# A decoder layer on one core: cross attention's sums stored straight into the rows of its output projection, the softmax shares spread by TensorE, the projection moved into the cross-attention stage, and the last down products dealt out

## The chip, the cores and the metric

One core of one Trainium2 chip. The metric is the device time of one execution in microseconds. Times of three runs of the kernel before: 1092.85, 1093.76 and 1097.8 us, median 1093.76.

## What is computed

A pre-norm decoder layer in float32 on x of shape 4 x 1024 x 256, 16 heads of 16. Only the last two of its three blocks matter here:

```python
x = x + self_attention(layernorm(x))
# cross attention, context of 77 rows, boolean mask
q, k, v = heads(layernorm(x) @ Wq), heads(ctx @ Wk), heads(ctx @ Wv)
attn = softmax(where(masked, -1e9, q @ k.T / 4))
x = x + (attn @ v).reshape(b, s, 256) @ Wo
# feed forward, hidden width 768
h = silu(n @ w_gate.T) * (n @ w_up.T)        # n = layernorm(x)
x = x + h @ w_down.T
```

## The kernel before, in words

The work runs in stages on one core: projections of self attention, self attention, a middle stage (its output projection and the queries of cross attention), cross attention (684 to about 849 us of the trace), feed forward (to the end). Tokens are held as 8 chunks of 512 (two to a batch), `xres` holds the residual of every chunk in SBUF. Matrix products that must be accurate are cut into three products of high and low parts (`cut_products`, line 128); line 135 is their one matmul.

**Cross attention** works in 16 groups, each 4 heads of one batch; groups 4b to 4b+3 are batch b. A group has 8 score units u (2 halves of 512 queries x 4 heads). For a unit TensorE makes the scores of 80 keys by 512 queries (lines 1339, 1341), ScalarE their exponentials (1301), and after each four units TensorE multiplies by the values (`products`, 1349). The value tile `vx` has VW = 32 columns to a head, 16 of values and 16 ones, so that a head's 32 rows of the PSUM bank are 16 sums and 16 equal softmax denominators. ScalarE copies them to `xu` (1293) and SP stores all of `xu` to DRAM, `od2` (1214). The maxima that the exponentials subtract are made two groups ahead: eight TensorE products (1324, 1326), each reduced by VectorE (1263), and two transposes `t` (1320) whose result VectorE copies to `xmrow` (1260) and SP moves under the queries (1209). These ten items go round a ring of three PSUM banks, so item N waits for VectorE's reading of item N-3. Their order, and their places between the score units, are the lists `ring2` and `plan2` (lines 1116 to 1130). The queries come by six DMAs to a group, three groups ahead (`load_cross`, 1201). All DMAs of the stage go through SP's one queue, in program order, and SP waits in order too (`cross_sync`, 1206). The weights of feed forward are loaded at groups 0, 1 and 6 (1172) and split by ScalarE and GpSimd (1182, 1184, 1190).

**From sums to projection.** After a batch's four groups SP loads the denominators back (`load_den2`, 1401), VectorE inverts them at the end of group 4b+5 (`inverse`, 1406), SP stores the inverses (1410), and from group 7 on loads sums and inverses, the inverses repeated 16 times, into `oin2` and `din2` (`load_ffn`, 1417, 1419). GpSimd multiplies the two (`quotients3`, 1425), TensorE projects with `xwo` (`project3`, 1454), VectorE adds to `xres` (1436) and takes the moments for the next norm. Chunk 0's projection stands in group 15; those of chunks 1 to 7 stand at the head of the feed-forward iterations.

**Feed forward**, iteration c of 8, on TensorE: the projection of chunk c+1, gate and up products of hidden tiles 2, 3, 4, the transposes of chunk c+1 (`turn`, 1571), tile 5, tiles 0 and 1 of chunk c+1, then the 72 down products of chunk c. A hidden tile goes TensorE, ScalarE (silu, 1549), VectorE (1500, 1502), GpSimd (the low part, 1475). The last iteration has only tiles 2 to 5 and the down products.

Of the kernel before, what the change touches and what calls it, by code (L numbers as in the profile page):

```python
# [29 lines left out]
def program(nc, x, ctx_t, mask_t, Wq, bq, Wk_t, bk, Wv_t, bv, Wo_t, bo, W_cross, shift_w, gate,  # L30
# [35 lines left out]
    od2 = dram("od2", (G, HG, 2, HD, S), F32)  # L66
    rdn2 = dram("rdn2", (G * HG, S), F32)
# [5 lines left out]
    with root:  # L73
# [36 lines left out]
        vx = sb(root, "vx", [SK, B, H, VW])  # L110
# [171 lines left out]
        def qkv_gpsimd(g):  # L282
# [26 lines left out]
            nc.gpsimd.memset(vx[0:S2, :, :, HD:VW], 1.0).then_inc(s_con, 1)  # L309
# [806 lines left out]
        ring2 = [("m", i) for i in range(8)]  # L1116
        ring2.insert(6, ("t", 0))
        ring2.append(("t", 1))
        NMX2, NST2, NPS2, LAG2, AHEAD, LATE2 = len(ring2), 2 * HG, 8, 3, 2, 2

        plan2, at = [], 0
        for u in range(NST2):
            plan2.append(("s", u, 0))
            if u == LATE2:
                plan2.append(("r", NMX2 - 1, AHEAD - 1))
            plan2 += [("p", half, -1) for half in range(2) if HG * (half + 1) - 1 == NST2 + u - LAG2]
            plan2 += [("p", half, 0) for half in range(2) if HG * (half + 1) - 1 == u - LAG2]
            upto = max(0, u + 1 - LATE2) * (NMX2 - 1) // (NST2 - LATE2)
            plan2 += [("r", n, AHEAD) for n in range(at, upto)]
            at = upto  # L1130
# [75 lines left out]
        def cross_sync(sp, first):  # L1206
            def maxima(g, c):
                sp.wait_ge(xs_mxe, g * NMX2 + ring2.index(("t", c)) + 1)
# [12 lines left out]
            for g in range(G):  # L1221
                if g + GB - 1 < G:
# [8 lines left out]
                if g < 2:  # L1231
                    load_weight(sp, g)
                if g == 6:
                    load_weight(sp, 2)
                b = g // GB - 1
                if b >= 0 and g % GB == 1:
                    for w in range(2):
                        sp.wait_ge(xus[w], 16 * 2 * (b + 1))
                    load_den2(sp, b)
                if b >= 0 and g % GB == 2:  # L1240
                    store_inverse(sp, b)
                if 7 <= g < 7 + 2 * KT:
                    load_ffn(sp, (g - 7) // KT, [(g - 7) % KT])
            store(G - 1)

        def cross_gpsimd(g):
            for x in range(3 * NPC):
                ffn_weight_low(g, x)
            for c in range(2):
                quotients3(g, c)  # L1250
            power3(g, 0)

        def cross_vector(v, first):
            def item(g, n):
                kind, m = ring2[n]
                N = g * NMX2 + n
                src = bank[MXB[N % NMB]]
                v.wait_ge(xs_mxf, N + 1)
                if kind == "t":
                    nc.vector.tensor_copy(xmrow[:, g % 2, m], src[0:32, 0:P // 2].bitcast(BF16)).then_inc(xs_mxe, 1)  # L1260
                    return
                half, r = m // 4, m % 4
                nc.vector.tensor_reduce(xpm[:, half, :, r], src[:, 0:HG * SK].rearrange("p (h w) -> p h w", h=HG),  # L1263
                                        AX, ALU.max).then_inc(xs_mxe, 1)
                if r == 3:
                    v.wait_ge(xs_mxe, N + 1)
                    top = xpm[:, half].rearrange("p h r -> p (h r)")
                    nc.vector.tensor_copy(xmt[:, half, 0], top).then_inc(xs_cmb, 1)
                    v.wait_ge(xs_cmb, 2 * g + half + 1)
                    nc.vector.tensor_tensor(xmt[:, half, 1], top, xmt[:, half, 0], ALU.subtract).then_inc(xs_mt, 1)  # L1270

            if first:
                for n in range(AHEAD * NMX2 - 1):
                    item(n // NMX2, n % NMX2)
                return
# [515 lines left out]
```

## Time and profile before

| what | value |
|---|---|
| median of 3 runs | 1093.76 us (1092.85 to 1097.8) |
| the profiled execution's own time | 1098.37 us |
| its span in the trace, first to last instruction | 1096.5 us |
| busy: TensorE, VectorE, ScalarE, GpSimd | 1036.7, 722.4, 577.0, 216.3 us |
| mean granted TensorE clock | 0.956 |
| chain that ended last, share of TensorE | 75% |

The page of the profile gives shares of the whole span; the stages have different limits, so the rows below are taken by stretch. In the trace "idle before <-X" on an instruction is how long its engine stood still before it and what ended that. Matmuls are pipelined: the distance from start to start is their cost, their own duration is longer. A float32 matmul stands as two records.

### The profile page before, as it was taken

The page shows a single profiled execution, that of the slowest core. Times are in us where ns is not written, and L with a number is a line of the kernel's source. Part 1 is how long each engine was busy: PE and PEld are TensorE (multiplying, and loading weights), DVE is VectorE, ACT ScalarE, POOL GpSimd, SP SyncE. Part 2 cuts the span into 40 slices and gives each one's busy share as a digit, 9 for nine tenths or more (in the row PEclk, how much of TensorE's full clock was granted, in tenths as well). Part 3 has the DMA queues.
Part 4 walks back from the last instruction along what each step waited for, and adds up shares of the span by engine and source line. Part 5 has one row for each costly group of instructions (what it writes and reads, how often), then busy time and mean ns, then how long its engine had stood idle before and what let it go on. Part 6 is the DMA issues. An engine that isn't in the chain of part 4 may idle for free.

```text
span 1096.5 us, 18966 instructions
## 1 busy us (share of the span) xinstructions
PE 1036.7 (95%) x7044; PEld 615.4 (56%) x7092; DVE 722.4 (66%) x1571; ACT 577.0 (53%) x1093; POOL 216.3 (20%) x228
## 2 busy tenths in 40 slices
PE   4999799999999999999999998999889999999997
PEld 3877244444444444444444465544334788888886
DVE  7877978777787788887785375655453545445552
ACT  4785167676676676676676577377555211111110
POOL 6655700000000000000000044011020233333431
PEclk9999599999999999999999999699888899999999
DMA  8589604444433344444400237588851111111101
GB/s 252 198 217 313 121 2 80 79 80 80 69 65 59 66 72 74 83 84 79 80 16 15 40 118 174 131 210 190 195 120 64 63 58 58 54 43 49 48 2 38
DMA packets 85511, 105.30 MB, mean 96 GB/s; under 512 B 12548, under 2 KB 73696, under 8 KB 83885
## 3 DMA queue, kind: packets, MB, share of 16 engines
q1 hardware_dynamic: 82907, 100.92, 39.1%
q10 hardware_dynamic: 2514, 3.18, 1.3%
q8 instruction: 56, 0.92, 0.4%
q14 instruction: 34, 0.28, 0.1%
HBM read 61.80 MB, written 37.06 MB: 90 GB/s over the span
## 4 chain that ended last, share of the span: by engine, by line
PE 75%; DVE 15%; ACT 4%; DMA 3%; issue 2%; SPq 1%; POOL 0%; POOLq 0%; DVEq 0%; ACTq 0%
PE bank L135 21%; PE bank L843 11%; PE bank L810 10%; PE bank L829 9%; DVE pm L740 8%; PE bank L1101 3%; PE bank L1454 3%; PE bank L1339 2%; PE bank L1341 2%; PE bank L941 2%; PE bank L1349 2%; PE bank L833 2%; PE bank L1324 2%; PE bank L815 2%; PE bank L1326 2%
## 5 line engine op out<-in xcount | busy, mean ns | idle before, releaser
L787 ACT ACTIVATE prob<-bank 128x512 f32<-128x512 f32 (+1 forms) x608 | 317.7, 584 | 188.5 <-PE bank L833 101.6
L740 DVE TENSOR_REDUCE pm<-bank 128x1 f32<-128x512 f32 (+3 forms) x608 | 356.9, 655 | 87.6 <-PE bank L815 66.8
L810 PE MATMUL bank<-stk,stq 96*128 96x512 bf16 (+3 forms) x768 | 226.1, 338 | 5.1 <-DVE pm L740 2.8
L829 PE MATMUL bank<-stq,stk 98*128 98x512 bf16 (+3 forms) x768 | 222.8, 331 | 2.6 <-ACT prob L787 0.5
L843 PE MATMUL bank<-prob,va 128*17 128x512 f32 (+3 forms) x1536 | 145.5, 497 | 2.5
L810 PEld LDWEIGHTS bank<-stk,stq 96*128 96x128 bf16 x768 | 68.7, 98 | 136.4 <-DVE pm L740 80.2
L1549 ACT ACTIVATE e_sg<-bank 128x512 f32<-128x512 f32 x48 | 28.7, 599 | 189.3 <-PE bank L135 189.3
L1301 ACT ACTIVATE xprob<-bank 80x512 f32<-80x512 f32 x128 | 72.4, 591 | 66.5 <-PE bank L1341 65.1
L961 POOL TENSOR_TENSOR c_rstd<-c_ve,mhalf 128x4 f32<-128x4 f32 x8 | 8.1, 1008 | 500.6 <-DVE c_ve L128 500.6
L829 PEld LDWEIGHTS bank<-stq,stk 98*128 98x128 bf16 x768 | 69.5, 99 | 45.0 <-ACT prob L787 9.2
L1263 DVE TENSOR_REDUCE xpm<-bank 128x4 f32<-128x320 f32 x128 | 58.9, 488 | 37.8 <-PE bank L1326 36.2
L843 PEld LDWEIGHTS bank<-prob,va 128*17 128x17 f32 x1536 | 40.5, 113 | 72.8 <-issue 52.8
L833 PE MATMUL bank<-tri_k,identb 128*128 128x128 bf16 (+1 forms) x335 | 80.3, 240 | 0.0
L135 PE MATMUL bank<-e_xnt,wg 128*128 128x512 f32 x288 | 77.0, 403 | 1.4 <-DVE e_xnt L1507 1.4
L1475 POOL TENSOR_TENSOR e_ht<-e_hf,e_ht 128x512 fp32r<-128x512 f32 x48 | 62.5, 1303 | 73.5 <-DVE e_ht L1502 73.5
L815 PE MATMUL bank<-tri_q,identb 128*128 128x128 bf16 (+1 forms) x321 | 76.0, 237 | 0.0
L135 PE MATMUL bank<-wd,e_ht 128*128 128x256 f32 x576 | 71.8, 286 | 3.2 <-POOL e_ht L1475 3.2
L135 PE MATMUL bank<-e_xnt,wu 128*128 128x512 f32 x288 | 74.5, 395 | 0.0
L135 PEld LDWEIGHTS bank<-wd,e_ht 128*128 128x128 f32 x576 | 71.4, 195 | 4.2 <-POOL e_ht L1475 3.6
L1500 DVE TENSOR_TENSOR e_hf<-bank,e_sg 128x512 f32<-128x512 f32 x48 | 33.1, 690 | 51.2 <-ACT e_sg L1549 51.2
L135 PEld LDWEIGHTS bank<-e_xnt,wg 128*128 128x128 f32 x288 | 54.6, 192 | 12.8 <-DVE e_xnt L1507 1.8
L135 PEld LDWEIGHTS bank<-e_xnt,wu 128*128 128x128 f32 x288 | 54.9, 191 | 11.8
(172 smaller groups left out, 1376.7 us busy)
## 6 DMA issues: line engine op xcount, KB each, us to landing
qk<-a_parts SPq DMA_DIRECT2D x32, 384.0 KB, 2.7
od<-xu SPq DMA_DIRECT2D x16, 512.0 KB, 4.0
xq<-c_parts SPq DMA_DIRECT2D x16, 384.0 KB, 3.1
xstq<-xq SPq DMA_DIRECT2D x32, 192.0 KB, 4.7
stq<-qk SPq DMA_DIRECT2D x30, 192.0 KB, 4.0
stk<-qk SPq DMA_DIRECT2D x15, 384.0 KB, 6.2
vs<-a_vst SPq DMA_DIRECT2D x8, 544.0 KB, 4.2
oall<-u_out SPq DMA_DIRECT2D x64, 64.0 KB
```

Of the source, the lines that this page charges most:

```text
L135: mm = nc.tensor.matmul(dst, a[:, i], b[:, j], start=(n == 0), stop=(n == 3 * len(terms) - 1))
L740: nc.vector.tensor_reduce(pm[:, k, h0:h0 + hb, r], src[:, 0:hb * w].rearrange("p (h w) -> p h w", h=hb), AX, ALU.max).then_inc(s_mxe, 1)
L787: nc.scalar.activation(prob[:, U % NPS, 0:hb * n], bank[STB[U % NSB]][:, 0:hb * n], ACT.Exp).then_inc(s_ex, 1)
L810: mm = nc.tensor.matmul(dst[:, h * w:(h + 1) * w], stq[i][0:R, half, h0 + h, r * P:(r + 1) * P], stk[i][0:R, h0 + h, k0:k0 + w], start=(h ...
L815: mm = nc.tensor.matmul(dst[:, 0:hb * w].rearrange("p (h w) -> p h w", h=hb)[:, :, w - P:w], identb[:], tri_q[:, 0:hb], start=False, stop= ...
L829: mm = nc.tensor.matmul(dst[:, h * n:(h + 1) * n], stk[i][0:RM, h0 + h, kt * P:(kt + 1) * P], stq[i][0:RM, half, h0 + h, q0:q0 + n], start ...
L833: mm = nc.tensor.matmul(dst[:, 0:hb * n].rearrange("p (h n) -> p h n", h=hb)[:, :, 0:P], identb[:], tri_k[:, 0:hb], start=False, stop=True ...
L843: mm = nc.tensor.matmul(bank[PVB[half]][h * VW:h * VW + VC, q0:512], va[g % NB][:, kt, :, h], prob[:, (g * NST + first + h // hb) % NPS, ( ...
L1263: nc.vector.tensor_reduce(xpm[:, half, :, r], src[:, 0:HG * SK].rearrange("p (h w) -> p h w", h=HG), AX, ALU.max).then_inc(xs_mxe, 1)
L1301: nc.scalar.activation(xprob[:, U % NPS2], bank[STB[U % NSB]][0:SK, :], ACT.Exp).then_inc(xs_ex, 1)
L1475: nc.gpsimd.tensor_tensor(ht[:, c % 2, 1, h], hf[:, h % 2], ht[:, c % 2, 0, h].bitcast(F32), ALU.subtract).then_inc(es_hl, 1)
L1500: nc.vector.tensor_tensor(hf[:, h % 2], bank[5 + 2 * (h % 2)][:], sg[:, h % 2], ALU.mult).then_inc(es_h, 1)
```

## The change

- The DRAM tensors `od2` and `rdn2`, their loads and GpSimd's quotients go. `store_sums3` writes each head's 16 rows of `xu` into the projection's rows `oall2` in SBUF, four DMAs of 64 KB to a group, and the denominators by a fifth into `den2`; before it was one DMA of 512 KB.
- The denominators of a batch are inverted and cut into three bfloat16 parts on VectorE (`shares3`), in unit 4 of group 4b+5, stored to DRAM and loaded as 48 rows. TensorE spreads them over the 16 rows of each head (`sel`, a matmul of 512 columns), VectorE multiplies.
- Spreads ("s") and half projections ("o") are items of the ring of three banks. Those of chunks 0 to 5 stand in groups 7, 11 and 15, two chunks to a group; those of chunks 6 and 7 in feed-forward iterations 1 and 2.
- The places of the other ring items shift by at most one within a unit. Chunk 0's moments and norm follow groups 13 and 14 on VectorE.
- The last two weight loads go from groups 1 and 6 to groups 3 and 7. `vx` has 17 columns to a head.
- The last chunk's down products are dealt between its gate and up products, 12 to a hidden tile, each waiting for its own tile.

```diff
+        def cross_items(g):
+            todo = [[] for u in range(NST2)]
+            b, i = g // GB - 1, g % GB
+            if b >= 0 and i == 3:
+                for u in range(2):
+                    todo[4 * u].append(("s", 2 * b + u, 0))
+                    todo[4 * u + 1].append(("s", 2 * b + u, 1))
+                    todo[4 * u + 2].append(("o", 2 * b + u, 0))
+                    todo[4 * u + 3].append(("o", 2 * b + u, 1))
+            if g + AHEAD - 1 < G:
+                todo[LATE2].append(("t", g + AHEAD - 1, 1))
+            if g + AHEAD < G:
+                ring = maxima_of(g + AHEAD)
+                for n, item in enumerate(ring):
+                    todo[LATE2 + n * (NST2 - LATE2) // len(ring)].append(item)
+            return todo
...
-            def store(g):
-                sp.wait_ge(xs_u, 2 * g + 2)
-                sp.dma_start(od2[g:g + 1].rearrange("a h w r t -> (a h w r) t"), xu[:, g % 2]).then_inc(xus[g % 2], 16)
...
                 if g:
-                    store(g - 1)
+                    store_sums3(sp, g - 1)
+                if b >= 0 and i == 1:
+                    store_shares3(sp, b)
                 if g + AHEAD < G:
                     maxima(g + AHEAD, 0)
...
+                if g in (0, 3, 7):
+                    load_weight(sp, (0, 3, 7).index(g))
+                if b >= 0 and i == 1:
+                    load_shares3(sp, b)
...
+                for u, due in enumerate(steps2[g]):
+                    if b >= 0 and i == 1 and u == 4:
+                        shares3(v, b)
...
+                if g == G - 3:
+                    moments3(v, 0)
+                if g == G - 2:
+                    normalise3(v, 0)
...
+                if kind == "s":
+                    t.wait_ge(s_rl2, 16 * (g // 2 + 1))
+                    nc.tensor.matmul(dst[:], sel[:, m], shares_of(g), start=True, stop=True).then_inc(xs_mxf, 1)
+                    return
+                if kind == "o":
+                    t.wait_ge(xs_mxe, place2["s", g, KT - 1] + 1)
+                    project3(dst, g, m).then_inc(xs_mxf, 1)
+                    return
...
+            sp.wait_ge(xs_u, 2 * g + 2)
+            for h in range(HG):
+                row = HD * (HG * (i % 2) + h)
+                sp.dma_start(oall2[row:row + HD, b % 2, i // 2],
+                             xu[h * VW:h * VW + HD, g % 2]).then_inc(xus[g % 2], 16)
+            rows = S // DT * HG
+            sp.dma_start(den2[rows * i:rows * (i + 1), b % 2],
+                         xu[HD:P:VW, g % 2].rearrange("a (c t) -> a c t", t=DT)).then_inc(xus[g % 2], 16)
...
+            nc.vector.reciprocal(den2[:, q], den2[:, q]).then_inc(s_rd2, 1)
+            for part in range(2):
+                v.wait_ge(s_rd2, n + 2 * part + 1)
+                nc.vector.tensor_copy(xr3[:, q, part], den2[:, q]).then_inc(s_rd2, 1)
+                v.wait_ge(s_rd2, n + 2 * part + 2)
+                if part == 0:
+                    nc.vector.tensor_tensor(den2[:, q], den2[:, q], xr3[:, q, 0], ALU.subtract).then_inc(s_rd2, 1)
+                else:
+                    nc.vector.tensor_tensor(xr3[:, q, 2], den2[:, q], xr3[:, q, 1], ALU.subtract).then_inc(s_rd2, 1)
...
             t.wait_ge(s_fl, 3 * NPC)
+            t.wait_ge(xs_mxe, NMX2)
             turn(0)
...
-            for c in range(NCH):
-                more = c + 1 < NCH
-                if more:
-                    project3(t, c + 1)
-                for h in range(2, HT - 1):
+            for c in range(NCH - 1):
+                if c in LATE_AT:
+                    spread3(c - 1)
+                gate_up(c, 2)
+                if c in LATE_AT:
+                    t.wait_ge(es_on, KT * c)
+                    for w in range(2):
+                        t.wait_ge(es_yo, 2 * (c - 1) + w + 1)
+                        project3(bank[OB[w]], N_LATE + c - 1, w).then_inc(es_op, 1)
+                for h in range(3, HT - 1):
                     gate_up(c, h)
...
                 down(c)
+            for h in range(HT):
+                if h + 2 < HT:
+                    gate_up(NCH - 1, h + 2)
+                down_part(NCH - 1, h)
```

## Rows read from the trace of the kernel before

**Rows 1.** The page, granted TensorE clock in 40 slices of 27.4 us.

```profile
PEclk9999599999999999999999999699888899999999
```

**Rows 2.** Busy time and clock by stretch: PE, PEld, DVE, ACT, POOL, PEclk, DMA share, GB/s.

```profile
730.00:738.10 8.10, 8.10 (x78) 3.84 (x74) 4.69 (x14) 6.29 (x13) 1.00 (x1) 1.00 0.76 161
784.00:788.00 4.00, 2.10 (x12) 1.05 (x12) 0.89 (x2) 1.08 (x2) 0.00 (x0) 0.59 0.97 224
841.40:1096.50 255.10, 243.98 (x1367) 212.77 (x1365) 123.12 (x265) 42.05 (x73) 84.74 (x62) 0.97 0.14 46
```

**Rows 3.** TensorE's timeline, the product with the values in several groups: start, us.

```profile
703.97 1.06 PE L1349 MATMUL bank<-xprob,vx 80*32 80x512 f32 x8
...
729.15 1.06 PE L1349 MATMUL bank<-xprob,vx 80*32 80x512 f32 x8
...
737.22 1.06 PE L1349 MATMUL bank<-xprob,vx 80*32 80x512 f32 x8
...
830.14 1.06 PE L1349 MATMUL bank<-xprob,vx 80*32 80x512 f32 x8
...
848.08 1.07 PE L1349 MATMUL bank<-xprob,vx 80*32 80x512 f32 x8 [0.77 <-ACT xprob L1301]
```

**Rows 4.** TensorE's timeline, its three long waits inside the cross stage.

```profile
784.86 0.45 PE L1324 MATMUL bank<-xstk,xstq 96*128 96x80 bf16 x4 [1.91 <-DMA xstq<-xq]
...
788.18 0.45 PE L1324 MATMUL bank<-xstk,xstq 96*128 96x80 bf16 x4 [1.23 <-DVE xmrow L1260]
...
822.35 0.27 PE L1320 MATMUL bank<-identb,xmt 128*32 128x128 bf16 x1 [4.01 <-DVE xmt L1270]
```

**Rows 5.** Waits of the stretch 684 to 842: us in total, times, longest.

```profile
PE bank L1324 <- DMA xstq<-xq: 3.5, 4, 1.9
```

**Rows 6.** VectorE's timeline at the second and third of them.

```profile
787.11 0.95 DVE L1406 RECIPROCAL den<-den 128x128 f32<-128x128 f32 x1 [5.50 <-DMA den<-od]
...
819.94 2.26 DVE L1270 TENSOR_TENSOR xmt<-xpm,xmt 128x16 bf16<-128x16 f32 x1
```

**Rows 7.** GpSimd's timeline at the third.

```profile
817.53 4.63 POOL L1425 TENSOR_TENSOR oin<-oin,din 128x1024 f32<-128x1024 f32 x2
```

**Rows 8.** Chain that ended last, in order of time: start, us, what (pieces of it).

```profile
630.77 0.54 PE bank L926 x2
...
853.95 8.50 PE bank L135 x24
...
865.90 8.20 PE bank L135 x36
874.10 0.87 PE bank L1571 x8
874.97 16.84 PE bank L135 x108
891.81 3.45 PE bank L1454 x16
```

**Rows 9.** SP's queue in one group of cross attention.

```profile
727.66 0.34 SPq L1214 DMA_DIRECT2D od<-xu  x1
730.56 0.62 SPq L1209 DMA_DIRECT2D xstq<-xmrow  x1
731.22 2.80 SPq L1201 DMA_DIRECT2D xstq<-xq  x6
```

**Rows 10.** Self attention's stores of one head, on SP: ns least, median, most.

```profile
L699 SPq DMA_DIRECT2D oall<-u_out x64: 519/588/1539, 169.0 to 624.0; - x64
```

**Rows 11.** VectorE's groups from 620 us on: sums of 512, pieces of the shares.

```profile
L1436 DVE TENSOR_TENSOR xres<-bank,xres 128x512 f32<-128x512 f32 x16 | 11.1, 692 | 22.2 <-PE bank L1454 22.2
L913 DVE CAST r<-den 128x128 bf16<-128x128 f32 x2 | 0.5, 230 | 0.1
L916 DVE TENSOR_TENSOR den<-den,r 128x128 f32<-128x128 f32 x1 | 0.3, 303 | 0.0
```

**Rows 12.** TensorE's timeline at the last down products.

```profile
1081.98 10.25 PE L135 MATMUL bank<-wd,e_ht 128*128 128x256 f32 x72 [3.21 <-POOL e_ht L1475]
```

More of the change, by code:

```diff
@@ L1356, in cross_tensor @@
                 t.wait_ge(xs_set, 32)
-                for n in range(AHEAD * NMX2 - 1):
-                    maxima(n // NMX2, n % NMX2)
+                for N in range(len(lead2)):
+                    item(N)
                 return
+            N = len(lead2)
             for g in range(G):
                 for what, which, ahead in plan2:
-                    if g == G - 1 and what == "s" and which == NST2 - 3:
-                        t.wait_ge(xs_mxe, G * NMX2)
-                        project3(t, 0)
                     if what == "s":
@@ L1369, in cross_tensor @@
                         products(g + ahead, which)
-                    elif what == "r" and g + ahead < G:
-                        maxima(g + ahead, which)
+                    elif what == "r":
+                        for _ in steps2[g][which]:
+                            item(N)
+                            N += 1
             for half in range(2):
@@ new lines, in sums_of, with shares_of, project3 @@
+        def sums_of(c, k):
+            return oall2[:, c // 2 % 2, k, c % 2 * CH:(c % 2 + 1) * CH]
+        def shares_of(c):
+            return rd2[:, c // 2 % 2, c % 2 * CH:(c % 2 + 1) * CH]
+        def project3(dst, c, w):
+            for i in range(2):
+                for k in range(KT):
+                    mm = nc.tensor.matmul(dst[:, i * D:(i + 1) * D], sums_of(c, k)[:, (2 * w + i) * P:(2 * w + i + 1) * P],
+                                          xwo[:, k], start=(k == 0), stop=(k == KT - 1))
+            return mm
@@ L1582, in gate_up, with spread3 @@
                 mm.then_inc(es_gu, 1)
+            def spread3(x):
+                t.wait_ge(s_rl2, 16 * B)
+                for k in range(KT):
+                    nc.tensor.matmul(bank[TB2[k]][:], sel[:, k], shares_of(N_LATE + x), start=True, stop=True).then_inc(es_bc, 1)
             def down(c):
                 t.wait_ge(es_hl, HT * (c + 1))
-                if c + 1 < NCH:
-                    t.wait_ge(es_x2, 2 * (c + 1) + 2)
+                if c in LATE_AT:
+                    t.wait_ge(es_x2, 2 * c)
                 for w in range(2):
+                    need(t, es_yo, 2 * (c - 1) + w + 1)
                     for i in range(2):
@@ L1593, in down, with down_part @@
                     mm.then_inc(es_y, 1)
+            def down_part(c, h):
+                if h == 0:
+                    t.wait_ge(es_yo, 2 * c)
+                t.wait_ge(es_hl, HT * c + h + 1)
+                for w in range(2):
+                    for i in range(2):
+                        tok = slice((2 * w + i) * P, (2 * w + i + 1) * P)
+                        for n, (x, y) in enumerate(((0, 0), (0, 1), (1, 0))):
+                            mm = nc.tensor.matmul(bank[OB[w]][:, i * D:(i + 1) * D], ht[:, c % 2, x, h, tok], wd[:, y, h],
+                                                  start=(h == 0 and i == 0 and n == 0),
+                                                  stop=(h == HT - 1 and i == 1 and n == 2), skip_group_check=True)
+                    if h == HT - 1:
+                        mm.then_inc(es_y, 1)
             t.wait_ge(s_fl, 3 * NPC)
+            t.wait_ge(xs_mxe, NMX2)
             turn(0)
```

227 lines of the change are left out of this document (104 added, 123 removed).

## Prediction

> **What bounds the kernel now.** I read the slices of the clock first, then the stretches, then the timeline of the engine that each stretch hangs on, and the chain that ended last for the end. TensorE bounds both stages that the change touches. In a steady group of cross attention it is busy for all 8.1 us, VectorE for 4.7 and ScalarE for 6.3; in feed forward it is busy for 244 of 255 us, VectorE for 123 and GpSimd for 85 [rows 2]. So what counts is TensorE's work, and the stretches where it stands still or gets half its clock. The slices show the second: from about 767 to 877 us the mean grant is 0.8 to 0.9 of full, and after that full again [rows 1].
>
> How much is lost there comes from one mark that every group sets. The product with the values in unit 6 stands at 729.15 and 737.22, so a quiet group takes 8.07 us; groups 0 and 13 set it at 703.97 and 830.14 [rows 3]. That is 126.2 us for 13 groups that would take 104.9: **21.3 us are lost**. TensorE's own long waits account for only 7.15 us of it (1.91, 1.23 and 4.01) [rows 4], and shorter waits for query loads for 1.6 more (3.5 in all, less the 1.91) [rows 5]. Nearly all the rest is half clock after them: between 784 and 788 us the grant has fallen to 0.59 [rows 2]. The second wait is for VectorE, which stood 5.50 us before the reciprocal until the denominators were back from DRAM [rows 6]. The third is for VectorE too: a subtraction of 16 columns, in SBUF, took 2.26 us [rows 6] while GpSimd's first two quotients ran, 4.63 us together [rows 7]. The first is for a query load, which shares SP's queue and the DMA engines with the reloading of sums and inverses.
>
> **The sum, part by part**, against the profiled execution's 1098.37 us.
>
> *Projections and spreads.* A chunk's projection costs TensorE 3.45 us wherever it stands [rows 8]. Five of them leave the feed-forward iterations and five enter groups 7, 11 and 15, all on TensorE's path: 0. The spreads are new, two to each of 8 chunks; two like them took 0.54 us [rows 8]: 16 x 0.27 = **+4.3**. VectorE's share is 8 products or sums of 0.69 us [rows 11] to a group of two chunks, 5.5 us, while that group grows by 2 x (3.45 + 0.54) = 8.0 us, so VectorE has room. The half projection in unit 2 needs the quotients of the spread in unit 1: TensorE has a score unit and a product between them, some 1.4 us, VectorE one product of 0.69. The three banks of the ring let TensorE be three items ahead. I cost these waits at nothing; if the cover failed, each of six pairs would cost about 0.7, +4 at most.
>
> *The cross stage's waits.* The reload of denominators, the quotients on GpSimd and the reloads of sums go, and the second and third weight loads come away from the crowded places. So go the second and third wait and their half clock, and I take it that the first goes as well. What is late next is the ordinary query load; I keep its 1.6 us [rows 5]. **-19.7**, with bounds 0 and -21.3.
>
> *The shares on VectorE.* In unit 4 of groups 5, 9 and 13 VectorE now makes a reciprocal of 0.95 us [rows 6], two casts of 0.23 and two subtractions of 0.30 [rows 11]: 2.0, with the waits between them about 2.3 us, ahead of the reduction on which the transpose in unit 6 hangs. TensorE has 2.4 us of other work before it needs that transpose; the reduction and its two small operations come to about 0.9 behind the shares. That leaves some 0.9 us of wait in each of three groups: **+2.7** (bounds 0 and, with half clock behind each, 20, see the rivals). Their fourth use, in feed-forward iteration 0, puts about 0.4 us before the first gate product of chunk 1: **+0.4**. The store and the reload of the shares, one DMA each, sit on SP between groups 5 and 6, 9 and 10, 13 and 14; the query load behind them starts some 2 us late and is wanted two groups later, after a spread and a half projection have been added there. Nothing.
>
> *SP's queue.* A group's SP work before was six query loads (2.80), two maxima (0.62 each) and one store (0.34) [rows 9]: 4.4 us. Now the store is four DMAs, such as self attention issues in 0.59 each at the median [rows 10], and one like the 0.62 of the maxima: 3.0 instead of 0.34, 7.0 in all, of 8.07. The store at 727.66 was followed by the next one only at 730.56, held by VectorE, 2.90 us later [rows 9]. The new store ends 0.1 us behind that. So SP is nearly full, but hides: 0.
>
> *The join of the stages.* Before, the last product ended at 849.15 [rows 3] and gates started at 853.95 [rows 8], 4.8 us later, with chunk 0's sums, moments, power and norm on the way. Now the norm is ready in group 14. What stays is the transposes, ScalarE's copies behind its last output, and VectorE's low part: 0.45 + 0.6 + 0.6 + 0.6 + 0.7, about 2.8: -2.0. The wait of 0.77 before the last product [rows 3] is covered by a half projection: -0.8. Together **-2.8**. The first 24 gate matmuls took 8.50 us instead of 24/36 of 8.20 = 5.5 [rows 8], half clock after idling. About 2 us of idling stay, and a wait of 1.91 was enough to bring half clock before [rows 4]; I leave these 3 us as they are.
>
> *The tail.* Before, after the last gate product TensorE stood 3.21 us and made the 72 down products in 10.25 [rows 12]: 13.5. In a full iteration 36 gate and 72 down products take 16.84, and 36 gate products 8.20, so 12 down products take 8.64/6 = 1.44 [rows 8]. Now three parts (4.3 us) go before the last gate products, two (2.9) fill the wait of 3.21, and one (1.44) follows: 4.3 + 3.2 + 1.44 = 8.9. **-4.6**, part of it because no half clock follows a wait of 0.3.
>
> Removing quotients from GpSimd in feed forward (2.3 us to a chunk [rows 7]) is worth nothing there: TensorE hides it, and every iteration still lasts its 25.9 us of TensorE work. Iterations 1 and 2 keep a projection. The down products need VectorE's output sums of the chunk before, long done.
>
> Sum: 4.3 - 19.7 + 2.7 + 0.4 - 2.8 - 4.6 = -19.7, so 1078.7 for an execution like the profiled one. That one lay 4.6 us above the median of the three runs shown; I apply the same difference to the median: 1093.76 - 19.7 = **1074.0 us**. If the extra 4.6 us were waits that the change removes, the median would gain only 15, 1078.7.
>
> **Rivals.**
>
> *New waits with half clock (1085).* Of the 21.3 us lost now, three waits of 7.15 brought about 12.5 us of half clock, some 4 us each. If the shares on VectorE hold TensorE for 2 us instead of 0.9 in two of the three groups, or a query load comes late as often, each costs 5 to 6 us more: 1074 + 11 = 1085. For it: the query loads are as many as before, and the DMA share is 0.76 even in a quiet group [rows 2]. Against: the new stores move 272 KB to a group, not 512, and the reloads are gone.
>
> *The stage's losses stay (1092).* If it is the query loads themselves that fill the DMA engines, and VectorE's waits only shadowed them, the 19.7 us come back in other places: 1074 + 18 = 1092, no change. Against: TensorE waited on queries for 3.5 us only, on VectorE for 5.2 [rows 4, 5].
>
> *SP's queue becomes the bound (1118, slower).* One mechanism: the five stores of a group issue slowly, and every query load behind them is late. Self attention's stores took up to 1.54 us to issue [rows 10]; at 1.54 each a group's SP work is 2.8 + 1.2 + 7.7 = 11.7, 3.7 over 8.07, over 12 groups 44 us: 1118. It decides from the point where the excess eats the gain, 20/12 = 1.7 us to a group, 1.14 us for each store. Against: the median is 0.59, in a stage of the same queue, though a quieter one. [...]
>
> **How the numbers follow.** The forecast gets 0.72 (its own range 1065 to 1082), new waits 0.15, losses that stay 0.07, SP 0.06. What a measurement of this kernel can tell is about 0.5%, 5.5 us. Below 1088.3 lie the first two cases: faster 0.87; the third is no change, 0.07; the fourth slower, 0.06. The range is 1065 to 1087: below, no half clock at the join (-3), no wait for the shares (-2.7) and none for queries (-1.6); above, the case of new waits.
>
> **What the profile after would show.** A grant of full clock from the start of the cross stage's quiet part to its end; the unit 6 mark 8.07 us apart in ordinary groups and about 16 in groups 7 and 11; no GpSimd instruction of 2.3 us; SP's five stores done in 3 us; gates starting under 3 us after the last product; iterations of 25.9 us with two of 29.9; the last down part alone behind the last wait. Wrong would be: a mark more than 9.5 us apart in groups 5, 9 or 13, query loads as a releaser for more than 4 us, or SP issuing without a pause.

## The result and the profile after

The kernel after takes **1077.62 us** (median of 20 runs, 1072.58 to 1091.39). The kernel before, beside it, takes 1090.16 (20 runs, 1087.87 to 1101.12). The ratio is 0.989, with a 95% interval of 0.987 to 0.991: faster by 12.5 us. The ratios here and below leave out single runs that lie over 1.5% above the fastest of the same kernel (1091.39 is one); medians and ranges keep them. The forecast was 1074.0 and faster; the time lies 3.6 us above it and inside the range.

The profiled execution of after took 1077.88 us, its span is 1076.2, its mean clock 0.978. Measured on the same marks as in the prediction, the two profiled executions compare so (us; "first mark" is the product with the values in unit 6 of group 0, and "gates" are the first gate products of feed forward; the forecast's column is the prediction's own terms, sorted by where they fall):

| stretch | before | after | difference | forecast |
|---|---|---|---|---|
| start to first mark | 703.97 | 701.73 | -2.2 | 0 |
| first mark to group 13's mark | 126.17 | 126.18 | 0.0 | -1.9 |
| group 13's mark to gates | 23.81 | 26.67 | +2.9 | +2.6 |
| gates to the end of the span | 242.55 | 221.62 | -20.9 | -20.4 |
| sum | 1096.5 | 1076.2 | -20.3 | -19.7 |

The forecast's terms: the second stretch takes in four projections (+13.8) and eight spreads (+2.2), loses 19.7 and gains 1.8 for the shares of groups 5 and 9; the third takes in the shares' wait of group 13, which stands behind that group's mark (+0.9), one projection and four spreads (+4.5), less 2.8 for the join; the last gives up five projections (-17.25), takes in four spreads (+1.1), loses 4.6 in the tail and gains 0.4. Read alone, the second stretch looks as if nothing happened: it holds 16 us more of TensorE's work in the same time.

The page of after, its busy row and its clock, slices of 26.9 us; the clock answers to [rows 1]:

```profile
PE 1028.1 (96%) x7108; PEld 604.0 (56%) x7108; DVE 726.8 (68%) x1603; ACT 576.6 (54%) x1093; POOL 197.1 (18%) x220
PEclk9999599999999999999999999799999999999999
```

The run of 8s of [rows 1] is gone. What is left is one 7 at 673 to 699 us, the way into the cross stage, where [rows 1] have a 6. Busy time by stretch shows what is left of waiting (PE, PEld, DVE, ACT, POOL, clock, DMA share, GB/s; the last row answers to the third of [rows 2]):

```profile
740.00:748.00 8.00, 6.95 (x63) 3.09 (x61) 5.92 (x18) 5.86 (x12) 0.99 (x1) 1.00 0.71 118
854.58:1076.20 221.62, 215.41 (x1244) 189.44 (x1244) 110.32 (x244) 36.02 (x63) 69.52 (x55) 1.00 0.07 22
```

The first stretch is group 5, where the shares are made: TensorE stands for 1.05 of 8 us, at full clock. TensorE's timeline has the marks in it, beside [rows 3], and the waits that took the place of [rows 4]:

```profile
701.73 1.05 PE L1377 MATMUL bank<-xprob,vx 80*17 80x512 f32 x8
...
726.26 1.05 PE L1377 MATMUL bank<-xprob,vx 80*17 80x512 f32 x8
...
734.23 1.05 PE L1377 MATMUL bank<-xprob,vx 80*17 80x512 f32 x8
...
742.58 1.05 PE L1377 MATMUL bank<-xprob,vx 80*17 80x512 f32 x8
...
744.58 0.22 PE L1348 MATMUL bank<-identb,xmt 128*32 128x128 bf16 x1 [0.95 <-DVE xmt L1288]
...
751.85 1.05 PE L1377 MATMUL bank<-xprob,vx 80*17 80x512 f32 x8
...
757.11 1.99 PE L1475 MATMUL bank<-xwo,oall 128*128 128x256 f32 x8
...
759.89 0.32 PE L1352 MATMUL bank<-xstk,xstq 96*128 96x80 bf16 x4 [0.24 <-DVE xres L1278]
...
827.91 1.05 PE L1377 MATMUL bank<-xprob,vx 80*17 80x512 f32 x8
...
850.92 1.05 PE L1377 MATMUL bank<-xprob,vx 80*17 80x512 f32 x8
...
854.58 1.66 PE L134 MATMUL bank<-e_xnt,wg 128*128 128x512 f32 x6 [1.57 <-DVE e_xnt L1543]
...
873.64 1.66 PE L134 MATMUL bank<-e_xnt,wg 128*128 128x512 f32 x6 [1.55 <-DVE e_xnt L1543]
...
1070.21 1.70 PE L1663 MATMUL bank<-wd,e_ht 128*128 128x256 f32 x12 [0.36 <-POOL e_ht L1513]
```

A quiet group takes 734.23 - 726.26 = 7.97 us. The wait at 744.58 is the forecast's 0.9, measured 0.95; with it group 5 takes 751.85 - 742.58 = 9.27. The last two rows are the wait that the forecast put at 0.4, and the last down part alone. TensorE's waits for query loads, beside [rows 5]:

```profile
PE bank L1352 <- DMA xstq<-xq: 0.8, 2, 0.5
```

SP's queue in one group, beside [rows 9]; then SP's own waits from 710 to 850 us:

```profile
729.39 2.96 SPq L1226 DMA_DIRECT2D xstq<-xq  x6
732.39 0.63 SPq L1234 DMA_DIRECT2D xstq<-xmrow  x1
733.06 2.45 SPq L1436 DMA_DIRECT2D oall<-xu  x4
735.55 0.61 SPq L1439 DMA_DIRECT2D den<-xu  x1
```

```profile
SPq L1234 <- DVE xpm L1281: 22.3, 16, 4.9
SPq L1436 <- ACT xu L1313: 11.8, 7, 5.2
```

The five stores are 2.45 + 0.61 = 3.06 us. This group has no pause on SP, but over the stage SP still waits for the other engines for over 34 us, so it is not what sets the pace.

And the chain that ended last, beside [rows 8]: one DMA of the denominators stands in it, the first 24 gate products ran at full clock (5.75 us for 8.50), and a full iteration's 144 products are 25.00:

```profile
735.55 5.84 DMA den<-xu
...
854.58 5.75 PE bank L134 x24
...
957.26 25.00 PE bank L134 x144
```

### The profile page after: what moved, and what is told of

Same layout as the page of the kernel before. It is cut to its first block, busy times and chain, and to the rows that moved or that the text cites. A ratio compares the mean times of both kernels' runs of the same rounds, so it can differ in the third digit from the quotient of the medians.

```text
span 1076.2 us, 19117 instructions
## 1 busy us (share of the span) xinstructions
PE 1028.1 (96%) x7108; PEld 604.0 (56%) x7108; DVE 726.8 (68%) x1603; ACT 576.6 (54%) x1093; POOL 197.1 (18%) x220
## 4 chain that ended last, share of the span: by engine, by line
PE 77%; DVE 15%; ACT 3%; issue 2%; DMA 2%; SPq 1%; POOL 0%; POOLq 0%; DVEq 0%; ACTq 0%
PE bank L134 19%; PE bank L842 12%; PE bank L809 11%; PE bank L828 10%; DVE pm L739 7%; PE bank L1475 3%; PE bank L1100 3%; PE bank L832 3%; PE bank L814 2%; PE bank L1367 2%; PE bank L940 2%; PE bank L1377 2%; PE bank L1369 2%; PE bank L1352 2%; PE bank L1354 1%
## 5 line engine op out<-in xcount | busy, mean ns | idle before, releaser
L814 PE MATMUL bank<-tri_q,identb 128*128 128x128 bf16 (+2 forms) x352 | 88.0, 250 | 0.0
L832 PE MATMUL bank<-tri_k,identb 128*128 128x128 bf16 (+2 forms) x352 | 86.7, 246 | 0.0
L134 PEld LDWEIGHTS bank<-wd,e_ht 128*128 128x128 f32 x504 | 61.4, 192 | 0.5
L134 PE MATMUL bank<-wd,e_ht 128*128 128x256 f32 x504 | 61.6, 283 | 0.0
```

What stands on the lines that cost most here:

```text
L134: mm = nc.tensor.matmul(dst, a[:, i], b[:, j], start=(n == 0), stop=(n == 3 * len(terms) - 1))
L814: mm = nc.tensor.matmul(dst[:, 0:hb * w].rearrange("p (h w) -> p h w", h=hb)[:, :, w - P:w], identb[:], tri_q[:, 0:hb], start=False, stop= ...
L832: mm = nc.tensor.matmul(dst[:, 0:hb * n].rearrange("p (h n) -> p h n", h=hb)[:, :, 0:P], identb[:], tri_k[:, 0:hb], start=False, stop=True ...
```

## The experiments

Eleven runs followed, in three sets, each on another chip, so times are compared with the kernel before of the same set.

**Before and after once more.** The profiled execution of before lay 8.2 us above its median over 20 runs. Were its losses typical?

> The kernel before, unchanged, in another execution. Theory T (the profiled execution was untypical): its median over 20 runs is 1090.2 us, the profiled one took 1098.4, so another execution loses some 8 us less than 21.3 over groups 0 to 13 of cross attention: the marks of groups 0 and 13 stand about 118 us apart instead of 126.2. Theory S (the losses are the same in every execution and the rest is spread over all stages): 126 us again.

Measured: 1090.21 us, and the loss was all there. First mark 698.91, then 125.73 us to group 13's mark, against 126.17. TensorE's timeline has the three waits of [rows 4] again: the first as 1.06 instead of 1.91, the second as 1.93 instead of 1.23, the third as 4.00 instead of 4.01, together 6.99 instead of 7.15:

```profile
779.01 0.32 PE L1324 MATMUL bank<-xstk,xstq 96*128 96x80 bf16 x4 [1.06 <-DMA xstq<-xq]
...
782.11 0.32 PE L1324 MATMUL bank<-xstk,xstq 96*128 96x80 bf16 x4 [1.93 <-DVE xmrow L1260]
...
816.32 0.26 PE L1320 MATMUL bank<-identb,xmt 128*32 128x128 bf16 x1 [4.00 <-DVE xmt L1270]
...
1075.11 8.89 PE L135 MATMUL bank<-wd,e_ht 128*128 128x256 f32 x72 [3.21 <-POOL e_ht L1475]
```

So the 21 us lost in the cross stage belong to the kernel, and not to one execution. The 8.2 us lie elsewhere: the first mark was 5.1 earlier, in stages that the change does not touch, and feed forward 2.7 shorter, with the first 24 gate products in 7.16 instead of 8.50 us and the last 72 down products in 8.89 instead of 10.25 [rows 8, 12].

> The kernel after, unchanged, in another execution. Its 20 runs reach from 1072.6 to 1091.4 us, with the mean clock falling from 0.982 to 0.963 as the time rises. Theory T: the extra time of a slower execution is half clock behind one or two waits in cross attention (groups 0 to 13 apart by more than the 126.2 us of the first profile); at a time near 1073 to 1078 us it is 123 to 127. Rival: the spread comes from the stages before 684 us, then this distance stays at 126 and the first mark moves from 701.7.

Measured: 1082.94 us, 5.1 above the first profile of after. First mark 699.04, but then **133.93** us to group 13's mark, not 126.18. TensorE's timeline, then its windows, then VectorE's and GpSimd's timelines:

```profile
743.44 0.26 PE L1348 MATMUL bank<-identb,xmt 128*32 128x128 bf16 x1 [2.06 <-DVE xmt L1288]
...
748.35 1.91 PE L1377 MATMUL bank<-xprob,vx 80*17 80x512 f32 x8
...
756.92 1.05 PE L1377 MATMUL bank<-xprob,vx 80*17 80x512 f32 x8
```

```profile
740.00:760.00 20.00, 17.88 (x101) 7.18 (x100) 10.27 (x30) 9.62 (x19) 1.99 (x2) 0.66 0.47 87
```

```profile
739.51 0.95 DVE L1456 RECIPROCAL den<-den 128x128 f32<-128x128 f32 x1 [0.73 <-DMA den<-xu]
...
742.08 1.01 DVE L1286 CAST xmt<-xpm 128x16 bf16<-128x16 f32 x1
```

```profile
742.07 0.99 POOL L1215 TENSOR_TENSOR wu<-iw,wu 128x384 fp32r<-128x384 f32 x1 [7.93 <-ACT wu L1209]
```

The wait for the shares was 2.06 us instead of 0.95, and behind it the clock was granted at 0.66 over 20 us; the product with the values took 1.91 instead of 1.05. Group 5's mark stands at 740.32 and the next at 756.92, 16.6 us apart instead of 9.27, over the 9.5 that the prediction named as a sign of being wrong. In all 7.75 us went, of which the longer wait itself is 1.11. Those 1.11 are two things. The denominators came later by 0.27: VectorE stood 0.73 us for them, and 0.46 in the first profile. And the cast that otherwise takes 0.17 us took 1.01, 0.84 more, since GpSimd had begun the low part of a weight 0.01 us earlier and worked for 0.99. In the first profile of after the same two missed each other by 0.10 us; VectorE's timeline and GpSimd's there:

```profile
741.49 0.95 DVE L1456 RECIPROCAL den<-den 128x128 f32<-128x128 f32 x1 [0.46 <-DMA den<-xu]
...
744.05 0.17 DVE L1286 CAST xmt<-xpm 128x16 bf16<-128x16 f32 x1
```

```profile
744.32 0.99 POOL L1215 TENSOR_TENSOR wu<-iw,wu 128x384 fp32r<-128x384 f32 x1 [7.35 <-ACT wu L1209]
```

**The tail undone.**

```diff
-            for c in range(NCH - 1):
+            for c in range(NCH):
...
-            for h in range(HT):
-                if h + 2 < HT:
-                    gate_up(NCH - 1, h + 2)
-                down_part(NCH - 1, h)
```

> The change without the dealt last down products: the 72 stand together behind the last hidden tile again. Theory (the tail's term of the prediction): 4.6 us slower than the kernel after, about 1082 us at the median, ratio to before 0.993; TensorE waits 3.2 us before the 72 products and some of them run at half clock. Rival (the products wait for the same last tile either way, so dealing gains only the half clock): 1.7 us, about 1079, ratio 0.990.

Measured: ratio to before 0.9918 (0.9889 to 0.9946), median 1082.86 (five runs, 1079.34 to 1097.28) beside 1091.05; gates to end 225.89 us against 221.62. TensorE's last products:

```profile
1062.98 10.38 PE L134 MATMUL bank<-wd,e_ht 128*128 128x256 f32 x72 [3.21 <-POOL e_ht L1513]
```

By the traces the tail is worth **4.3 us**, 4.6 forecast. The ratios, from different sets, differ by 0.3%, some 3 us, and their intervals overlap. The wait for the shares was 0.51 here, and first mark to group 13's mark 125.77.

**The shares in three pieces**, behind units 4, 5 and 6 of the group, and in feed-forward iteration 0 behind the norm of chunk 1 and hidden tile 5:

```diff
-                    if b >= 0 and i == 1 and u == 4:
-                        shares3(v, b)
...
+                    if b >= 0 and i == 1 and u in (4, 5, 6):
+                        shares3(v, b, [u - 4])
...
-                if c == 0:
-                    shares3(v, B - 1)
...
+                if c == 0:
+                    shares3(v, B - 1)
```

> The change with VectorE's share work cut into three pieces that follow units 4, 5 and 6 of groups 5, 9 and 13 instead of standing together before the items of unit 4, and, in feed forward, moved behind the hidden tile 5 of iteration 0. Theory: TensorE's waits for these shares go, 1.7 + 0.75 + 0.4 us in cross attention and 1.55 us before the first gate product of chunk 1, 4 us together: 1073.6 us, ratio 0.985. Rival (the waits are filled from elsewhere, since VectorE works as much as before): groups 5 and 6 together stay over 17 us, and the time stays at 1077, ratio 0.989.

Measured: **0.9826** (0.9798 to 0.9854), median 1072.12 beside 1091.05, and five runs within 3 us. No wait for the shares is left, gates to end are 219.85 instead of 221.62, and group 13's mark to gates 25.93 instead of 26.67. But in group 5 another wait came up, for queries, at full clock:

```profile
739.71 0.32 PE L1352 MATMUL bank<-xstk,xstq 96*128 96x80 bf16 x4 [1.55 <-DMA xstq<-xq]
```

So in group 5 one wait took the place of the other: group 4's mark to group 6's is 17.57 us (733.64 to 751.21), where after had 17.62, and the rival's sign, over 17 us, was met there. The gain of this profile lies in groups 9 and 13 and in feed forward.

**The weight loads where before had them.**

```diff
-                if g in (0, 3, 7):
-                    load_weight(sp, (0, 3, 7).index(g))
+                if g in (0, 1, 6):
+                    load_weight(sp, (0, 1, 6).index(g))
```

> The change with the second and third weight loads back at groups 1 and 6. Theory: in group 5 VectorE's shares come late because the denominators of group 3 land behind the 768 KB of the load issued at group 3 (VectorE waited 0.46 and 0.73 us for them, TensorE 0.3 to 0.9 for queries just before), and where TensorE's wait reaches 2 us, half clock costs some 7 us; with the load gone from there group 5's wait is 0.4 us as in groups 9 and 13, no execution has half clock there, and the median falls from 1077.6 to about 1075, with the highest below 1082. Rival (the shares' own 2.3 us on VectorE make the wait): 0.9 us stay in group 5, and the executions spread over 1072 to 1091 us as before.

Measured: 0.9864 (0.9846 to 0.9883), median 1076.49, none of the four runs above 1078.27. In group 5 the denominators are there in time, and the wait is 0.40:

```profile
743.66 0.22 PE L1348 MATMUL bank<-identb,xmt 128*32 128x128 bf16 x1 [0.40 <-DVE xmt L1288]
```

So the 768 KB load of group 3 lengthens the wait in group 5, by making the denominators late (5.84 us in the chain above). It does so by way of the DMAs between: the load, issued at 728.94, had landed after 5.3 us, before the denominators' store was issued at 735.55, but query loads issued behind it, which take some 5.5 us each, were still under way. Windows of after, then of this run:

```profile
736.00:740.00 4.00, 3.70 (x33) 1.64 (x32) 1.75 (x7) 2.53 (x5) 0.97 (x1) 1.00 1.13 182
```

```profile
736.00:740.00 4.00, 4.00 (x39) 1.91 (x38) 2.12 (x7) 2.64 (x6) 0.97 (x1) 1.00 0.60 121
```

With the load at group 3 the DMA engines' share is 1.13 while the store is out, without it 0.60. That load's new place was part of the change, and I had counted it in its favour. This run does not tell the collision apart: here too a low part on GpSimd begins soon behind the cast (743.95, the cast ended at 743.30). But on a wait of 0.40 the 0.84 us of a collision would make 1.24, less than the 1.57 after which the clock stayed full in after.

**Both together.** The two edits above in one kernel.

> The spread shares of the run before (median 1072.1) together with the weight loads at groups 1 and 6. Theory: what is left there is a query wait of 1.55 us in group 5 from the load at group 3; it goes, and waits of 0.5 us come in groups 2 and 3 as in the kernel before: 1071 us, ratio 0.982, at most 1 us better than without. Rival: the early loads cost as much as they save, 1072 to 1073.

Measured: 0.9831 (0.9807 to 0.9855), four runs of 1070.20 to 1077.04 and a fifth of 1162.39, at a mean clock of 0.837, of which there is no trace. The ratio does not tell this kernel from the one with spread shares alone (0.9826). The traces do. Group 4's mark to group 6's, us (two quiet groups are 15.94):

| | shares in one piece | in three pieces |
|---|---|---|
| load at group 3 | 17.62 (after) | 17.57 |
| load at group 1 | 16.70 | 15.96 |

With both edits no wait over 0.2 us is left there, neither for shares nor for queries. The profiled execution took 1077.04 all the same, the longest of the four: its first mark and the next stand at 699.83 and 714.34, 14.51 us apart instead of 7.97, and from 690 to 710 us the clock was 0.50, with no wait of TensorE. The half clock with which every profile enters the cross stage lasted one group longer, some 6.5 us.

**Before, with GpSimd's quotients in pieces of 128 columns.**

```diff
-            nc.gpsimd.tensor_tensor(oin2[:, u], oin2[:, u], din2[:, u], ALU.mult).then_inc(es_on, 1)
+            for k in range(KT):
+                for part in range(4):
+                    o, d = (w[:, u, k, part * P:(part + 1) * P] for w in (oin2, din2))
+                    mul = nc.gpsimd.tensor_tensor(o, o, d, ALU.mult)
+            mul.then_inc(es_on, 1)
```

> The kernel before, GpSimd's quotients of a chunk as eight instructions of 128 columns instead of one of 1024. Theory (GpSimd holds what VectorE's small cast and subtraction need, for the length of one instruction): the two take at most 0.4 us each instead of 2.2, TensorE's wait of 4.0 us in group 13 falls under 1 and the half clock behind it goes: 7 us faster, 1083 us, ratio 0.993. Rival (VectorE is held for as long as GpSimd works, whatever the pieces): 2.2 us each again, no change.

Measured: 0.9953 (0.9919 to 0.9986). GpSimd works longer in all (6.66 us for 16 pieces against 4.63 [rows 7]), and yet the first cast and subtraction of 16 columns that VectorE makes beside it are short (the subtraction was 2.26 us [rows 6]), and TensorE's wait of 4.01 [rows 4] is 0.23. GpSimd's timeline, VectorE's and TensorE's:

```profile
819.34 6.66 POOL L1428 TENSOR_TENSOR oin<-oin,din 128x128 f32<-128x128 f32 x16
```

```profile
819.52 0.30 DVE L1268 CAST xmt<-xpm 128x16 bf16<-128x16 f32 x1
819.86 0.38 DVE L1270 TENSOR_TENSOR xmt<-xpm,xmt 128x16 bf16<-128x16 f32 x1
...
824.23 1.80 DVE L1268 CAST xmt<-xpm 128x16 bf16<-128x16 f32 x1
```

```profile
820.38 0.22 PE L1320 MATMUL bank<-identb,xmt 128*32 128x128 bf16 x1 [0.23 <-DVE xmt L1270]
```

Group 12's mark to group 13's is 8.39 us, where before has 15.31 (814.83 to 830.14). First mark to group 13's mark is 125.94 even so, as this profiled execution, the second slowest of its ten, lost 14.50 - 7.98 = 6.5 us at half clock between its first two marks and had waits of 1.00, 1.49 and 2.18 in groups 9 and 10, where before has 0.64, 1.91 and 1.23.

What held the first cast and subtraction was the length of one GpSimd instruction: each ends with the piece beside it. The cast at 824.23 does not fit that. It took 1.80 us, four times the 0.45 of a piece, and ended at 826.03, where GpSimd's last piece had ended at 826.00. So pieces shorten what GpSimd does to VectorE in some places and not in all; what decides it was not found. The Trainium skill, "SBUF — State Buffer" (Who interferes with whom), calls the port pair that the two engines share an exclusive lock, held for a whole instruction; by that rule a short VectorE instruction waits for the rest of a GpSimd one. The trace agrees for the two (2.26 us to 0.38), and for the later cast only if GpSimd's next piece got the pair first several times over, which no row shows.

**Before, with the inversion and its store one group later.**

```diff
-                if b >= 0 and g % GB == 2:
+                if b >= 0 and g % GB == 3:
...
-                if b >= 0 and g % GB == 1:
+                if b >= 0 and g % GB == 2:
```

> The kernel before with the inverse of a batch's denominators one group later (groups 6, 10, 14), and its store one group later on SP. Theory: VectorE no longer waits 5.5 us for the reload in group 9, TensorE's second wait (1.2 to 1.9 us) goes; if it was this wait that made the half clock of groups 10 and 11, some 10 us go as well: 1080 us, ratio 0.991. Rival: the query wait just before it (1.06 to 1.91 us) brings the half clock by itself, and only 1 to 2 us go.

Measured: 0.9967 (0.9948 to 0.9986), median 1087.80 beside 1091.64. VectorE no longer stands before the reciprocals of groups 6 and 10, and first mark to group 13's mark is 122.81. But in group 9 a query load is late, and half clock follows it; TensorE's timeline, windows, and SP's own waits:

```profile
774.50 0.45 PE L1324 MATMUL bank<-xstk,xstq 96*128 96x80 bf16 x4 [3.86 <-DMA xstq<-xq]
```

```profile
772.00:782.00 10.00, 7.50 (x46) 3.81 (x47) 3.31 (x8) 3.03 (x6) 0.00 (x0) 0.66 0.92 217
```

```profile
SPq L1417 <- DMA rdn<-den: 3.0, 1, 3.0
```

SP stood 3.0 us for the stored inverses before it could load them, and the queries behind it came late. One wait gave way to another on the same queue.

**The spread shares and after again, side by side.** The first comparison of the two was across sets.

> The spread shares again, beside the unchanged kernel after on the same chip. Theory (VectorE's shares in one piece are what makes the kernel after slow in some executions): the median is 1072 us again, no execution above 1078, and the kernel after stands 3 to 6 us higher with a spread of 10 us or more. Rival (the first comparison was luck of five executions): both spread alike and differ by no more than 2 us.

> The kernel after, unchanged, beside the spread shares. Theory: median 1076 to 1080 us, some executions above 1080, those with half clock behind group 5. Rival: 1072 to 1074 like the other.

Measured: spread shares 0.9867 (0.983 to 0.990), median 1077.00 (1076.69 to 1078.88); after 0.990 (0.986 to 0.994), median 1081.38 (1075.45 to 1087.28); before 1092.46. The medians lie 4.4 us apart, but with four and six runs the intervals overlap, and spread shares were not at the 1072 that was expected. The profiled execution of after was its longest, with the same picture as the second profile: first mark to group 13's mark 132.99, the cast at 0.90 us instead of 0.17 with GpSimd's 0.99 us begun 0.12 before it, and VectorE's wait for the denominators 0.85 instead of 0.46. The two differences, 0.73 and 0.39, make up the wait's 1.12 us. TensorE's timeline, windows, and the two others:

```profile
747.69 0.27 PE L1348 MATMUL bank<-identb,xmt 128*32 128x128 bf16 x1 [2.07 <-DVE xmt L1288]
```

```profile
740.00:760.00 20.00, 17.88 (x120) 8.04 (x120) 10.26 (x27) 9.31 (x19) 0.99 (x1) 0.69 0.69 120
```

```profile
746.43 0.90 DVE L1286 CAST xmt<-xpm 128x16 bf16<-128x16 f32 x1
```

```profile
746.31 0.99 POOL L1215 TENSOR_TENSOR wu<-iw,wu 128x384 fp32r<-128x384 f32 x1 [6.97 <-ACT wu L1209]
```

Spread shares had a query wait in group 5 again, of 2.60 us, and the clock over the same 20 us of the trace was 0.91. Group 4's mark to group 6's is 20.27 there and 24.62 in after.

**After with 32 columns to a head in `vx`**, as before had them. The ones fill the 15 columns more.

```diff
-        vx = sb(root, "vx", [SK, B, H, VC])
+        vx = sb(root, "vx", [SK, B, H, VW])
...
-                    mm = nc.tensor.matmul(bank[PVB[half]][h * VW:h * VW + VC, :], vx[:, b, i * HG + h],
+                    mm = nc.tensor.matmul(bank[PVB[half]][h * VW:(h + 1) * VW, :], vx[:, b, i * HG + h],
```

> The change with 32 columns to a head in the value tile again (16 sums and 16 equal denominators to a head). A quiet group takes 7.97 us after the change and 8.07 before. Theory A (the 17 columns shorten the weight load or the product): 8.07 comes back. Theory B (it is the transpose that no longer stands between score units and product): 7.97 stays. The time moves by at most 1.6 us.

Measured: 1073.79 us in one execution, gates to end 221.61. The marks, in TensorE's timeline, are 8.00 us apart, as against 7.97 with 17 columns and 8.07 before:

```profile
705.76 1.06 PE L1377 MATMUL bank<-xprob,vx 80*32 80x512 f32 x8
...
713.76 1.07 PE L1377 MATMUL bank<-xprob,vx 80*32 80x512 f32 x8
```

So the columns give 0.03 us to a group, and 0.07 of the 0.10 are left to what else changed in a quiet group, such as the places of the ring's items. What it is was not singled out.

## Why the prediction was right, and where its terms were off

**The mechanism held.** The waits for the reloaded denominators and for GpSimd's quotients went, and their half clock with them: the cross stage took in 16 us of work in the same 126.2 us. That the two waits were caused as I said is shown apart from the change: pieces on GpSimd removed the third wait, a later inversion the second. Neither alone gave over 5.8 us of median, since the other wait stayed and, for the inversion, a query load became late. Which part of the change freed the first, the query wait, was not run apart.

*Projections 0, spreads 4.3.* Over the two groups of a pair, 7 with 8 and 11 with 12, the marks stand 25.69 apart, 9.75 more than two quiet groups, where 8.0 was forecast. That is 1.8 too much for each pair and 3.5 for the two, the largest miss of a term inside the cross stage and near the +4 that was given as its bound. Two spreads and a projection are there cut into four items between bfloat16 scores; the half projections at 757.11 and 760.62 took 1.99 and 1.89 us, 3.88 together against 3.62 of busy time where one stands whole, and TensorE waited 0.24 for `xres` besides. In the chain, from start to end, they are 1.94 and 1.73, 1.92 and 1.80, where a projection that stands whole is 3.45, and a spread took 0.32 (754.41 to 754.73) for 0.27. In each pair of groups that makes 0.5 for the halves, 0.2 for the spreads and 0.24 for the wait; the other 0.8 of each pair were not singled out. So the cover against waits held nearly, and what was mis-sized is the work itself, priced as it costs where it stands whole. The unit 6 marks around groups 7 and 8 are 13.87 and 11.82 apart, not the 16 for group 7 that the prediction named. In feed forward, where they stand together, they cost what was forecast: the iterations with a projection took 30.09, forecast 29.9, the others 25.88.

*The cross stage's waits, -19.7.* Right for the second and third wait. Queries cost TensorE 0.8 us (two waits) where 1.6 was kept.

*The shares, +2.7.* In the first profile they cost 0.95 in group 5 and 0.40 in groups 9 and 13, 1.75 in all. But in two of the five profiles of kernels with these shares and this place of the loads the wait was 2.06 and 2.07, and 7.75 and 6.81 us were lost. This is the first rival, "new waits with half clock", in one of the three groups of an execution and at a little over its price of 5 to 6 us. After's 20 runs spread over 19 us; nine lie above 1079.8, each with a mean clock of at most 0.976, and the other eleven, below 1077.9, have at least 0.977. Not all of that is this wait: the first mark alone stood between 697.8 and 704.3 in the profiles, and in two of the thirteen, of other kernels, the half clock at the entry of the cross stage lasted one group longer and cost 6.5 us. How many of the nine longer executions were of which kind was not seen, as only the profiled ones have a trace. The step that failed is the forecast's one value for a wait that has several: it was sized from VectorE's own instructions, without the weight loads that the change moves, which make the denominators late, and without GpSimd's low parts of those weights, 0.99 us each, of which one can fall on the cast. The collision is read from both cases and from none of the other three; no run forced it. That the shares in one piece make the wait for shares is shown by the runs with three pieces, where it is gone; that the load at group 3 lengthens it, and puts a query wait of 1.55 or 2.60 in its place once the shares are spread, by the two runs with the load moved.

*Iteration 0, +0.4.* It was 1.55. The norm of chunk 1 (2.41 us) and then the shares stood on VectorE ahead of the low part that the gates wait for; I had set the shares against TensorE's room and forgotten that the norm uses it up. With the shares moved behind, gates to end fell by 1.8.

*SP's queue, 0.* Right. Four stores issued in 2.45 us, 0.61 each, near the 0.59 of [rows 10], and the fifth in 0.61. The third of the rivals fell. A store takes longer to land than to issue (the last landed 5.84 us after its issue), but SP does not wait for that: from 736.95, before it had landed, SP issued the next query loads.

*The join, 2.8.* The last product ended at 851.97 and gates began at 854.58, 2.6 us. The 3 us of half clock that I left standing were gone as well: 1.57 us of wait did not bring it.

*The tail, 4.6.* 4.3 by the tail undone. Against the before of most executions it is less, as its last 72 down products took 8.89 and not 10.25.

**The size.** The sum of -19.7 against the profiled execution came out at -20.3, though 2.2 of that is from stages that the change does not touch. So near a match is partly luck, as the misses offset each other: +3.5 in the projections' groups against -1.3 from 13 quiet groups that are each 0.10 shorter, and -2.75 of half clock at the join, which the sum left standing, against +1.2 in iteration 0 and +0.3 in the tail. Against the median it was 12.5, 7.2 less than forecast. That the time is only 3.6 us above the forecast is luck too: the three runs of before from which the forecast started had a median 3.6 us above that of the 20. The step that failed there is the last of the sum, where -19.7 was put on the median. The text had named the case (if what lay above the median were losses that the change removes, the median would gain less), and 2.7 us of it were: half clock in feed forward that the second run of before does not have. Another 1.7 us are the terms by stretch in the table above (+1.9, +0.3, -0.5) and 0.4 is before's own cross stage (125.73 for 126.17). The other 2.4 us lie within what the first mark varies, and were not separated.

The best kernels are the two with the shares in three pieces, with 0.9826 and 0.9867 in two sets and, with the loads of before, 0.9831 in one. Their ratios do not tell them apart; by the traces the second has no wait left in group 5.

## What to carry to other kernels

When work is moved off one engine, look at what shares a port, a queue or a bank with the place it goes to, and for waits of about 2 us ask how often they happen, not only how long they are: here 0.1 us between two instructions decided on some 7 us. Cut a block of VectorE work that stands ahead of something TensorE waits for into pieces, and put them behind the operations that it waits for. Take the sum against the execution that was profiled, but do not carry onto the median what only that execution lost. And when a wait goes, see what the engine waits for next: spread shares alone left group 5 as long as it was.

## What the runs showed of the hardware that was not expected

In the cross stage the clock stayed full after waits of 1.55 us (shares in three pieces) and, at the join, 1.57 (after). After the waits of 2.06 and 2.07 it was 0.66 and 0.69 over 20 us, and after one of 2.60 for queries 0.91. So the longer wait need not cost more. In before, half clock followed a wait of 1.91 too [rows 4], and at the join it came with three waits of 0.77, 1.45 and 1.41 within 7 us, each shorter than the 1.57 of after. What followed the wait of 2.06 cost 6.2 us, three times the wait itself.

A small VectorE instruction can cost many times itself: the cast and subtraction of 16 columns took 0.17 us alone, 0.90 and 1.01 beside a GpSimd instruction of 0.99, 0.30 and 0.38, but once 1.80, beside many of 128 columns, and 2.26 beside one of 1024.

A store of 16 KB took 5.84 us to land, at a DMA share of 1.13, when a load of 768 KB had been issued 6.6 us ahead of it on the same queue, though the load itself had landed; SP's issue time was unchanged at 0.61.
